# Stacked-row LoRA packing, resident A, reordered first loads and GpSimd low halves in the MLP of a four-layer kernel

## The reference

```python
def lora_add(base, inp, A, B):
    Ab = A[layer_idx][lora_indices]
    Bb = B[layer_idx][lora_indices]
    t = jnp.einsum('bri,bni->bnr', Ab, inp)
    return base + jnp.einsum('bor,bnr->bno', Bb, t) * SCALE
gate = lora_add(jnp.einsum('bnh,fh->bnf', x, W_gate), x, A_gate, B_gate)
up = lora_add(jnp.einsum('bnh,fh->bnf', x, W_up), x, A_up, B_up)
act = jax.nn.silu(gate) * up
x = x + lora_add(jnp.einsum('bnf,hf->bnh', act, W_down), act, A_down, B_down)

kc = k_cache[block_table].reshape(bsz, L, HK, D)     # 16 pages of 32 keys per sequence
vc = v_cache[block_table].reshape(bsz, L, HK, D)
o = softmax(scores(rope(rmsnorm(q)), concat(kc, k))) @ concat(vc, v)
x = x + einsum('bse,de->bsd', o, Wo)                 # 32 query heads, 8 key heads
x = x + x @ (quantized(W2 + delta) + delta).T        # delta = lora_B @ lora_A * 0.5
x = x + einsum('bsi,boi->bso', x, W3[adapter_ids])
```

## Time and profile before

| what | us |
|---|---|
| median of 3 timed runs | 1535.65 (1533.48 to 1535.83) |
| the profiled execution | 1530.62 |
| its span, first to last instruction | 1528.9 |
| granted TensorE clock, mean | 0.992 of full |
| PE busy | 1434.5 (94%) |
| DVE, ACT, POOL busy | 1163.2 (76%), 939.4 (61%), 493.7 (32%) |
| first matmul | 22.63 |
| unit 1 of the MLP begins on PE | 41.83 |
| half switch (`lora_down(10)`) | 129.52 |
| MLP tail and turn of x end, attention in step | about 300 |
| first seven attention units, one | 19.3 |
| later attention units, one, mean | 17.8 |

### The profile page before, as it was taken

One profiled execution on the slowest core, in us unless ns is written; L12 is line 12 of the kernel. 1 busy time (PEld: TensorE's weight loads), 2 busy tenths in 40 slices (PEclk: granted clock), 3 DMA queues, 4 the chain that ended last, 5 costly groups with the idle time before them and its releaser, 6 DMA issues.

```text
span 1528.9 us, 29324 instructions
## 1 busy us (share of the span) xinstructions
PE 1434.5 (94%) x8014; PEld 1230.2 (80%) x8014; DVE 1163.2 (76%) x2800; ACT 939.4 (61%) x1860; POOL 493.7 (32%) x678
## 2 busy tenths in 40 slices
PE   3998999788999899999999999999999999999988
PEld 2776887667788788888878887888788888888767
DVE  4675767566688788778878886888788778888756
ACT  2333232356677677767767776777677667777643
POOL 4243000155543333333433333343333333433200
PEclk9999999999999999999999999999999999999999
DMA  8678642345321112111111111021112111111214
GB/s 179 207 240 283 197 150 89 98 126 159 111 63 49 50 29 63 60 40 49 50 47 45 57 56 51 29 63 49 51 29 63 60 40 49 50 42 36 97 60 161
DMA packets 104275, 131.03 MB, mean 86 GB/s; under 512 B 11861, under 2 KB 79590, under 8 KB 98838
## 3 DMA queue, kind: packets, MB, share of 16 engines
q1 hardware_dynamic: 98678, 109.49, 23.6%
q0 software_dynamic: 5024, 17.93, 3.9%
q10 hardware_dynamic: 384, 1.41, 0.7%
HBM read 125.63 MB, written 36.72 MB: 106 GB/s over the span
## 4 chain that ended last, share of the span: by engine, by line
PE 75%; issue 9%; DVE 7%; ACT 2%; POOL 2%; DMA 2%; POOLq 1%; SPq 1%; ACTq 0%; DVEq 0%
PE proj_ps L1170 16%; PE sc L1210 12%; PE o_ps L1247 12%; PE proj_ps L1268 11%; PE ring L1229 8%; PE proj_ps L1026 4%; PE o_ps L1026 4%; PE sc L1026 3%; PE ring L1283 2%; PE ring L1295 1%; PE ring L1026 1%; DMA wd_raw<-in_WdT 1%; POOLq L584 1%; DVE w_l L1426 1%; POOL v_pages L585 1%
## 5 line engine op out<-in xcount | busy, mean ns | idle before, releaser
L1699 DVE TENSOR_TENSOR pTl<-ring,pTh 128x512 fp32r<-128x512 f32 x320 | 215.1, 689 | 72.8 <-ACT pTh L851 69.3
L833 ACT ACTIVATE p_sb<-p_sb,bias,rstd 128x640 f32<-128x640 f32 x256 | 235.8, 921 | 46.7 <-DVE bias L1675 46.7
L637 POOL TENSOR_TENSOR rstd<-var,half_neg 128x4 f32<-128x4 f32 x64 | 80.6, 1259 | 532.1 <-DVE var L1736 483.5
L851 ACT ACTIVATE pTh<-ring 128x512 fp32r<-128x512 f32 x320 | 184.4, 599 | 55.2 <-PE ring L1229 54.4
L1665 DVE CUSTOM_DVE_ANT_0 p_sb<-sc,mask 128x640 f32<-128x640 f32 x256 | 209.1, 817 | 4.4 <-PE sc L1210 0.8
L1229 PE MATMUL ring<-ident,p_sb 128*128 128x128 f32 x1280 | 183.5, 274 | 5.7 <-DVE p_sb L1691 3.4
L1170 PE MATMUL proj_ps<-wh,xh 128*128 128x512 f32 (+1 forms) x512 | 179.7, 351 | 8.9 <-issue 8.2
L1229 PEld LDWEIGHTS ring<-ident,p_sb 128*128 128x128 f32 x1280 | 153.9, 141 | 33.5 <-DVE p_sb L1691 3.7
L1170 PE MATMUL proj_ps<-wl,xh 128*128 128x512 f32 (+1 forms) x512 | 172.6, 337 | 0.0
L1170 PE MATMUL proj_ps<-wh,xl 128*128 128x512 f32 (+1 forms) x512 | 172.2, 336 | 0.0
L1210 PE MATMUL sc<-kTh,qTh 128*128 128x320 f32 x512 | 163.5, 319 | 1.8 <-DVE kTl L1800 1.8
(11 more groups left out here) (247 smaller groups left out, 3632.7 us busy)
## 6 DMA issues: line engine op xcount, KB each, us to landing
k_pages<-in_k_cache SPq DMA_DIRECT2D x128, 128.0 KB, 3.4
v_pages<-in_v_cache POOLq DMA_DIRECT2D x128, 128.0 KB, 3.5
k_raw<-k_pages SPq DMA_DIRECT2D x64, 256.0 KB, 3.1
v_raw<-v_pages SPq DMA_DIRECT2D x64, 256.0 KB, 3.0
stage<-in_Wqkv SPq DMA_DIRECT2D x32, 384.0 KB, 3.5
w_raw<-in_WguT SPq DMA_DIRECT2D x20, 512.0 KB, 5.7
stage<-in_WoT SPq DMA_DIRECT2D x32, 256.0 KB, 3.3
w_raw<-in_W3T SPq DMA_DIRECT2D x8, 1024.0 KB, 5.4
```

The source lines that it names most:

```text
L833: act_e.activation(p_sb[:, p_slot(u, h), :], p_sb[:, p_slot(u, h), :], ACT.Exp, bias=bias[:, h:h + 1], scale=rstd[:, u.k % 2, h:h + 1], ac ...
L851: act_e.activation(pTh[:, c, :], ring[c % 2][:, :], ACT.Copy).then_inc(S["pth"], 1)
L1699: v.tensor_tensor(pTl[:, c, :], ring[c % 2][:, :], pTh[:, c, :].bitcast(F32), ALU.subtract).then_inc(S["ptl"], 1)
```

## The change

1. Adapters are packed per pair of sequences. The 32 rows of a pair are stacked three times on 96 rows: `tb` holds t's high, low and high part, `wb` holds B's high, high and low part. One matmul then makes all three products of a pair, so `lora_out` is 2 matmuls of 256 columns for 3 of 512, and the last step of `down` 4 for 12. `lora_in` has 24 matmuls of 256 columns, `lora_down` 6 of 256. ACT fills the stack by 4 copies of 32x256 per unit (6 in the second half) for one of 128x256, DVE by 2 of 32x256.
2. A is loaded once for both halves, into its own `la_h`, `la_l`, and not again at the half switch.
3. First loads in another order: x chunk 0, the gate half of W block 0, the other x chunks, the up half, then A with W block 1 in the middle; the indices go to ACT's queue, B to GpSimd's. TensorE starts with `gate_base(0)`, `up_base(0)` and only then `lora_in`.
4. From q = 2 on the low half of W is made by GpSimd (`low_w`, one subtraction of 128x1024), each followed by 5 value-page copies.
5. In the first seven attention units GpSimd issues 4 value copies, not 8, and between k_sin and the rstd of k. SP copies keys 4 per MLP unit and 8 in seven attention units.
6. The angles and their reduction go from before unit 0 to units 1 and 2; masks to 3, rotary tables and codebook to 4, the parts of `weight2` one to two units later each. The fill of tails with zeros goes.

The core of the diff:

```diff
-            for n in range(2, 2 + 2 * EARLY):
-                pool.wait_ge(S["gate_up"], 2 * n + 1)
-                copy_values(8 * (n - 2), 8 * (n - 1))
+            def low_w(q):
+                w = P if q % FC < FC - 1 else FTAIL
+                pool.wait_ge(S["w_hi"], q + 2)
+                pool.tensor_tensor(w_l[:, q % 2, :, :, 0:w], w_blocks(q % 2)[:, :, :, 0:w],
+                                   w_h[:, q % 2, :, :, 0:w].bitcast(F32), ALU.subtract).then_inc(S["w_lo_pool"], 1)
+            for q in range(2, 2 * FC):
+                low_w(q)
+                copy_values(5)
...
+                if u.turn is None and u.k < B - 1:
+                    copy_values(4)
+
                 pool.wait_ge(S["k_var"], u.count(1, 1))
...
                 split_v(u + -1)
-                if u.turn is None and u.k < B - 2:
-                    copy_values(8 * (2 * EARLY + u.k), 8 * (2 * EARLY + u.k + 1))
...
-                three((gate_ps, up_ps)[k], [((w_h[:, q % 2, k, C, :], w_l[:, q % 2, k, C, :]), (tb_h[:, k, :], tb_l[:, k, :]))],
-                      False, True).then_inc(S["gate_up"], 1)
+                for j in range(2):
+                    ts = slice(j * 2 * T, (j + 1) * 2 * T)
+                    i = mm((gate_ps, up_ps)[k][0:w, ts], wb[0:STACK, n % 2, j, k, 0:w], tb[:, k, ts], start=False, stop=j == 1)
+                i.then_inc(S["gate_up"], 1)
...
+            gate_base(0)
+            up_base(0)
             lora_in(0, 0)
             lora_in(0, 1)
-            for n in range(FC):
+            lora_out(0, 0)
+            lora_out(0, 1)
+            for n in range(1, FC):
                 gate_up(n)
...
             for n in range(1, FC):
                 low_act(n - 1)
-                split_w(n + 2)
+                low_wb(n + 1)
                 if n >= FC - 3:
                     split_wd(n - (FC - 3))
                 if n == 1:
+                    angles()
+                    reduce_angles(0)
+                elif n == 2:
+                    reduce_angles(1)
+                elif n == 3:
                     masks()
-                elif n == 2:
+                elif n == 4:
                     rotary_tables()
-                elif n == 3:
                     codebook()
-                elif n < 9:
-                    weight2(0, n - 4)
-                elif n == FC - 1:
-                    weight2(1, 0)
+                for part in PARTS.get(n, ()):
+                    weight2(*part)
                 gated(n)
```

More of the change, by code:

```diff
@@ L285, in cond_resid_kernel @@
         w_in = [sem(f"w_in_{n}") for n in range(2)]
+        w_first = [sem(f"w_first_{k}") for k in range(2)]
+        xT_in = [sem(f"xT_in_{c}") for c in range(C)]
+        adapter_in = [sem(f"adapter_in_{n}") for n in range(2)]
         wd_in = [sem(f"wd_in_{n}") for n in range(3)]
@@ L407, in _ @@
                      ins["BdT"][bass.ds(adapter(b), 1), :, :].rearrange("a r f -> (a r) f"), S["lbd_in"])
-            for q in range(4, CH):
+            for q in range(4, 2 * FC):
                 load_w(q)
-                if q == 5:
+                if q == 7:
                     load_group(0)
@@ L738, in silu @@
             def silu(n):
+                r = rows(n % FC)
                 act_e.wait_ge(S["gate_up"], 2 * n + 1)
@@ L1041, in lora_in @@
                 for c in range(C):
-                    if k == 0:
+                    if hf and k == 0:
                         pe.wait_ge(S["xh_set"], C * hf + c + 1)
                         pe.wait_ge(S["xl_set"], C * hf + c + 1)
-                    i = three(bank, [((w_h[:, q % 2, k, c, :], w_l[:, q % 2, k, c, :]), (xT_h[:, c, :], xT_l[:, c, :]))],
-                              c == 0, c == C - 1)
-                i.then_inc(S["t_done"], 1)
+                    for j in range(2):
+                        ranks = slice((2 * hf + j) * PAIR, (2 * hf + j + 1) * PAIR)
+                        ts = slice(j * 2 * T, (j + 1) * 2 * T)
+                        a_h, a_l = la_h[:, k, c, ranks], la_l[:, k, c, ranks]
+                        for n, (a, x) in enumerate(((a_h, xT_h), (a_h, xT_l), (a_l, xT_h))):
+                            i = mm(bank[0:PAIR, ts], a, x[:, c, ts], start=c == 0 and j == 0 and n == 0, stop=c == C - 1 and j == 1 and n == 2)
@@ new lines, in lora_in, with base @@
+                i.then_inc(S["t_done"], 1)
+            def base(n, k):
+                m = n % FC
+                w = rows(m)
+                bank = (gate_ps, up_ps)[k]
+                for c in range(C):
+                    if n == 0 and k == 0:
+                        pe.wait_ge(S["xh_set"], c + 1)
+                        pe.wait_ge(S["xl_set"], c + 1)
+                    three(bank[0:w, :], [((w_h[:, n % 2, k, c, 0:w], w_l[:, n % 2, k, c, 0:w]), (xT_h[:, c, :], xT_l[:, c, :]))],
+                          c == 0, False)
@@ L1049, in gate_base @@
             def gate_base(n):
-                hf, m = divmod(n, FC)
-                q = hf * CH + m + 1
-                pe.wait_ge(S["w_hi"], q + 1)
-                pe.wait_ge(S["w_lo"], q + 1)
                 if n:
+                    wait_w(pe, n)
                     pe.wait_ge(S["silu"], n)
-                three(gate_ps, [((w_h[:, q % 2, 0, c, :], w_l[:, q % 2, 0, c, :]), (xT_h[:, c, :], xT_l[:, c, :]))
-                                for c in range(C)], True, False)
+                else:
+                    pe.wait_ge(S["w_hi"], 1)
+                    pe.wait_ge(S["w_lo"], 1)
@@ L1059, in up_base @@
+                base(n, 0)
             def up_base(n):
-                hf, m = divmod(n, FC)
-                q = hf * CH + m + 1
                 if n:
                     pe.wait_ge(S["act_f"], n)
-                three(up_ps, [((w_h[:, q % 2, 1, c, :], w_l[:, q % 2, 1, c, :]), (xT_h[:, c, :], xT_l[:, c, :]))
-                              for c in range(C)], True, False)
+                else:
+                    wait_w(pe, 0)
+                base(n, 1)
             def lora_out(n, k):
@@ L1082, in lora_down @@
                 hf, m = divmod(n, FC)
+                r = rows(m)
                 pe.wait_ge(S["act_lo"], n + 1)
@@ L1086, in lora_down @@
                     pe.wait_ge(S["t_masked"], 3)
-                i = three(lad_ps, [((lad_h[:, n % 2, :], lad_l[:, n % 2, :]), (act_h[:, m, :], act_l[:, m, :]))],
-                          m == 0, m == FC - 1)
+                for j in range(2):
+                    ts = slice(j * 2 * T, (j + 1) * 2 * T)
+                    a_h, a_l = (a[0:r, n % 2, j * PAIR:(j + 1) * PAIR] for a in (lad_h, lad_l))
+                    for k, (a, x) in enumerate(((a_h, act_h), (a_h, act_l), (a_l, act_h))):
+                        i = mm(lad_ps[0:PAIR, ts], a, x[0:r, m, ts], start=m == 0 and j == 0 and k == 0, stop=m == FC - 1 and j == 1 and k == 2)
                 i.then_inc(S["lad_used"], 1)
```

501 lines of the change are left out of this document (276 added, 225 removed).

## The result

| | before | after |
|---|---|---|
| median, us | 1534.57 (1533.12 to 1535.83) | 1574.31 (1571.52 to 1578.37) |
| ratio | | 1.0261, 95% interval 1.0236 to 1.0287 |
| span of the profiled execution | 1528.9 | 1569.8 |
| granted TensorE clock, mean | 0.992 | 0.962 |

The prediction was 1528 with a range from 1500 to 1541. It was wrong in sign and outside its range.

The account below looks back on a forecast made before the run. TensorE was taken as the bound outside start and switch, until DVE is late. Locked: -4.4 (start, units, switch, second half) + 3.6 clock + 2.6 correction - 9 attention = -7.2 from 1535.65, so 1528; range 1500 to 1541.

Parts of the forecast that it names:

- two falls of the clock: TensorE dropping to the low clock after waits, 1.8 us each, 3.6 in all in the locked case.
- the 2.6: Added because the same unit-by-unit sum for the kernel before came out 2.6 us too early in the first half.
- The lock (5): GpSimd's 2.4 us subtraction excludes DVE from SBUF: DVE waits 1.8 us every unit; unit 10 starts at 126, not 112.5.
- (a): The forecast case, port locked between DVE and GpSimd: 1528 us (1522 to 1536), chance 0.50.
- Rival (b): Port free or mild, as DVE's PSUM-reading and scalar operations may leave it free: 1506 us (1500 to 1511), chance 0.33.
- DVE in the second half (4, 5): Second half of the MLP: 104.1 us becomes 95.5 free, 102.5 locked, with only units 12 and 13 over TensorE's 9.34.
- ACT's small copies (1, 4): Packing saves TensorE about 20 us, nothing in the tail; DVE's cycle is 3.6 us plus the unit's piece.
- rival c: Units 1 to 13: lock and low clock together, 1.8 us per fall, twelve more falls give +14, 1550 us; chance 0.15.
- The start (2): First loads reordered: unit 1 starts at 35.4 instead of 41.83 us, gain 6.4, bounds 4 and 9.
- The switch (3): Half switch: A's second load, its 5.24 us wait and the low clock go; 29.1 becomes 21.2 us, gain 7.9.
- Early attention (6): First seven attention units: fewer GpSimd copies end TensorE's 11.4 us wait for q_cos; gain 9, bounds 5.5 and 12.
- Rival (d): Early copies delay the rstd of k beyond its slack, losing 3.5 to 9 us; locked 1532 to 1537; no separate chance.

Follow-up runs that it names:

- e1: Changed kernel with the low half of W made by DVE again, GpSimd keeping only its copies: 1554.76 us, ratio to before 1.0111.
- e11: Changed kernel, low W on DVE, angles during A's wait, W_down split behind act_h(10), early copies behind k's rstd, 90 instructions ahead of ACT's loop: 1510.57 us.
- e2: Kernel before with only the value copies changed, 5 per MLP unit and 4 ahead of the rstd of k: 1534.24 against 1535.72 us, ratio 0.9986.
- e8: Changed kernel, low W on DVE, W_down split behind silu(10), B's copies ahead of act_h, early copies behind k's rstd, 90 instructions ahead of ACT's loop: 1520.45 us.
- e12: Kernel before, MLP untouched, with early value copies behind the rstd of k and 60 more instructions ahead of ACT's loop: 1514.52 us, ratio 0.9867.

## Why the prediction was wrong, point by point

By the rows of the table the prediction had -6.4 at the start, +17.7 in units 1 to 10 (11.5, two falls of the clock and the 2.6), -7.9 at the switch, -1.6 in the second half, -9 from the tail to the seventh attention unit and nothing behind it. The runs showed -7.6, +19.3, -1.2, +14.5, -0.4 and +16.3. So two steps failed most: the second half, where DVE's chain was taken to have slack (16 us), and ACT's loop, which was in no term (16 us). The early copies (9 us) and the switch (7 us) follow.

- **The lock (5).** Right in mechanism and in its price per event (1.8 us; 2.4 for the subtraction). The forecast (a) was the right case. But act_l was to stand in every unit, and it did in six; in the others it was another DVE operation. Rival (b) was right that operations that read PSUM go free, and wrong for the scalar ones. What the lock cost in all was some 20 us (e1). In units 1 to 10 it took 15.2 us (98.8 against 83.6 in e1) where I had 13.4; in units 12 to 21 7.1, where I had 7, but on another base (next point).
- **DVE in the second half (4, 5).** This step failed by 16 us. I let a unit cost the longer of TensorE's 9.34 and DVE's cycle and found two units over. TensorE's being busy 104.05 of 104.1 said only that it was just the bound. DVE's waits of the kernel before, 150 to 254 us, say how near DVE was:

```profile
DVE w_l L1424 <- ACT w_h L694: 11.9, 9, 4.0
DVE e_sb L1567 <- PE proj_ps L1026: 7.0, 3, 2.6
DVE act_l L1544 <- ACT act_h L702: 7.0, 10, 0.7
```

  DVE waited for TensorE 7.0 us only, in three units. From the gated product of unit 14 to that of unit 18 it was 42.1 us, for 41.9 of matmuls, and DVE waited for TensorE 2.6 of them; the rest was its own work and its waits for ACT. So of the 8.6 us taken from TensorE at most about 7 could show, and each us put on the chain gated, act_h, act_l, copies of B, low_wb, piece, gated counts soon after. Predicted 95.5 free and 102.5 locked; measured 107.8 to 109.0 free (e11, e1) and 116.1. Counted as in the table, the kernel before has 101.6, and 104.1 in the prediction's stretch.
- **ACT's small copies (1, 4).** I costed low_wb on DVE and left ACT's four and six copies out of the cycle of 3.6 us; DVE waited 26.9 us for them in the changed kernel, 12.2 in e1. In the tail, "nothing" was a wait of 2.2 us [the row on L1171 above], whose cause the row doesn't name, and the low clock behind it. The early copies alone made the tail's row 4 us longer as well (e2), so the share of that wait in its 5.5 isn't known. The four matmuls of that step have 512 columns, and the prediction priced them at 256: 1.8 us saved and not 2.25.
- **The clock (rival c).** Its mechanism came beside the lock's: 78 slow matmuls against 10, at most 13 us, where I took 3.6. It was given 0.15, and put in units 1 to 13 with a sum of +14; the MLP lost 25 us up to unit 21 (-7.6 + 19.3 - 1.2 + 14.5), of which the clock's own share isn't shown.
- **The start (2).** Right: -7.6 at unit 0 (bounds 4 to 9). The terms of that step add up to 34.0 and not to the 35.4 that it gives; the last adapter matmuls of unit 0 started at 33.5. All but 1 us of the gain was given back in units 1 and 2, into which the angles had moved.
- **The switch (3).** The price was right, 21.12 in e11, the cause incomplete: behind A's load stood the slot of wd_h, 1.2 us later in the same row of ACT. It could have been read in the trace of before.
- **Early attention (6).** -9 predicted; -5.9 in the units, +4.9 ahead of the first rstd of q (e2): -1.5. Rival (d), the rstd of k, is what happened; TensorE's slack of 3.0 was taken from the eighth unit, and in the first two TensorE of the changed kernel waited 5.0 and 3.6 for k_cos. With the copies behind the rstd of k the seven units took 120.0 (e8) and 118.0 (e12), so the price of the copies had been larger than the 10.5 of the prediction. Its 17.8 for a unit without copies was a mean with the six long turns in it.
- **The turns of the loop.** In no term: +16. The diff changes nothing in ACT's loop, only the number of instructions ahead of it. The prediction had rows of the first, the eighth and the 64th unit, and none of a turn.

The sum of what the runs show: lock 20 (uncertain by 5 or so), ACT's loop 17, and the rest, some 3 us, is what is left of the 39.7: the chain of small copies and the moved pieces, less what the packing, start and copies give. How the rest splits between packing and pieces was not run, and so it stays open which of the two keeps the new MLP behind the old one in e11.

## What to carry to other kernels

A TensorE that is busy 100% of a stretch may have a second engine right behind it: add up that engine's own chain, waits between its neighbours included, over several units, before taking matmuls away. Moving a large elementwise operation from DVE to GpSimd needn't relieve DVE when both work in SBUF: here DVE lost 1.8 us of standing for each 1.2 us of work that it was spared. Where a kernel has a hardware loop, look at each engine's idle time behind the jump back, before and after an edit ahead of the loop. And where a wait is to be removed, look for what else the same instruction, and the one behind it, waited for.
